# The first head pair's rows from three queues, and routing and shared rows over two groups

## The reference

```
q, k, v = heads(xn @ Wq.T), heads(xn @ Wk.T), heads(xn @ Wv.T)      # 16 heads of 16
scores  = q k^T / 4
gauss   = exp(-0.5 |x - position|^2 / scale^2)     # 8 splats per head, of q and of k
dir     = tanh((x - position) . direction)
splat   = (amp qg) kg^T + strength (amp qg qd) (kg kd)^T
std     = softmax(causal(scores)) v Wo
gsa     = softmax(causal(scores + sensitivity splat)) v Wo
attention = (1 - blend) std + blend gsa

s = sqrt(softplus(xn @ gate_w.T));  two experts of 16 by top-k(s + gate_b);  weights s / sum
each expert takes its first 128 tokens: silu(x W1) * (x W3) @ W2      # inner width 176
plus a shared expert of the same form over all tokens
```

## Time and profile before

| | |
|---|---|
| median of 3 runs | 376.65 us (376.22 to 376.99) |
| the profiled execution | 378.75 us, span 376.9 us |
| PE busy | 334.7 us, 89% |
| PE weight loads busy | 174.8 us, 46% |
| DVE busy | 230.7 us, 61% |
| ACT busy | 194.1 us, 51% |
| POOL busy | 65.7 us, 17% |
| mean granted clock of TensorE | 0.947 |

### The profile page before, as it was taken

One profiled execution on the slowest core, in us unless ns is written; L12 is line 12 of the kernel. 1 busy time (PEld: TensorE's weight loads), 2 busy tenths in 40 slices (PEclk: granted clock), 3 DMA queues, 4 the chain that ended last, 5 costly groups with the idle time before them and its releaser, 6 DMA issues.

```text
span 376.9 us, 6181 instructions
## 1 busy us (share of the span) xinstructions
PE 334.7 (89%) x2172; PEld 174.8 (46%) x2172; DVE 230.7 (61%) x614; ACT 194.1 (51%) x278; POOL 65.7 (17%) x82
## 2 busy tenths in 40 slices
PE   0999996788979999999999999999999999989965
PEld 0643663343345544554455445544554454335433
DVE  4555857587674665567556655766577558776222
ACT  1699824525414365436543654366346547767530
POOL 7200140400047530110111011102010007710000
PEclk9999768598979999999999999999999999999995
DMA  6408623304341354245655565547555525510011
GB/s 220 131 0 103 107 38 41 60 13 60 47 135 15 41 75 73 71 89 102 142 153 105 113 139 153 107 93 154 129 125 111 79 53 127 143 42 2 0 57 56
DMA packets 27330, 33.01 MB, mean 88 GB/s; under 512 B 6593, under 2 KB 20097, under 8 KB 27297
## 3 DMA queue, kind: packets, MB, share of 16 engines
q1 hardware_dynamic: 23745, 28.32, 37.4%
q0 software_dynamic: 2128, 4.22, 3.9%
q10 hardware_dynamic: 1424, 0.04, 0.2%
HBM read 15.60 MB, written 4.28 MB: 53 GB/s over the span
## 4 chain that ended last, share of the span: by engine, by line
PE 72%; DVE 14%; ACT 9%; issue 3%; DMA 1%; SPq 0%; DVEq 0%; ACTq 0%
PE ps L817 16%; PE ps L745 9%; PE ps L800 8%; PE ps L788 7%; PE ps L754 7%; PE ps L718 6%; ACT arena_p L636 6%; DVE mx L1093 5%; PE ps L676 4%; PE ps L773 2%; PE ps L695 2%; PE ps L758 2%; PE ps L791 2%; DMA acc<-in_x_dram 1%; ACT small L641 1%
## 5 line engine op out<-in xcount | busy, mean ns | idle before, releaser
L636 ACT ACTIVATE arena_p<-ps 128x1024 f32<-128x1024 f32 (+1 forms) x192 | 147.2, 811 | 79.4 <-PE ps L800 53.7
L1093 DVE TENSOR_REDUCE mx<-ps 128x1 f32<-128x512 f32 (+3 forms) x160 | 89.3, 590 | 33.2 <-PE ps L718 22.7
L817 PE MATMUL ps<-arena_p,v_full 128*32 128x512 f32 (+3 forms) x768 | 72.6, 496 | 0.6 <-ACT arena_p L636 0.6
L718 PE MATMUL ps<-stage 96*128 96x512 bf16 (+3 forms) x160 | 51.5, 362 | 7.1 <-DVE mx L1093 4.7
L788 PE MATMUL ps<-stage 98*128 98x512 bf16 (+1 forms) x192 | 51.9, 337 | 4.7 <-ACT arena_p L636 4.2
L800 PE MATMUL ps<-stage 98*128 98x512 bf16 (+1 forms) x192 | 47.4, 332 | 3.0 <-ACT arena_p L636 2.4
L641 ACT ACTIVATE small<-ps 128x176 f32<-128x176 f32 x24 | 7.6, 318 | 64.1 <-PE ps L745 64.1
L387 POOL DMA_INDIRECT wt<-xn_scratch,ids_sb x16 | 15.2, 951 | 133.2 <-PE ps L735 127.6
L817 PEld LDWEIGHTS ps<-arena_p,v_full 128*32 128x32 f32 x768 | 20.2, 110 | 35.4 <-issue 30.3
L754 PE MATMUL ps<-arena_o,small 88*128 88x256 f32 x96 | 27.4, 409 | 8.3 <-DVE small L1116 6.3
L788 PEld LDWEIGHTS ps<-stage 98*128 98x128 bf16 x192 | 18.8, 100 | 23.5 <-ACT arena_p L636 9.8
(11 more groups left out here) (193 smaller groups left out, 418.5 us busy)
## 6 DMA issues: line engine op xcount, KB each, us to landing
w_sb<-in_w_dram SPq DMA_DIRECT2D x16, 352.0 KB
stage<-split SPq DMA_DIRECT2D x48, 96.0 KB, 2.9
stage<-split SPq DMA_DIRECT2D x48, 64.0 KB, 2.7
arena_o<-in_w_dram SPq DMA_DIRECT2D x16, 176.0 KB
stage<-split SPq DMA_DIRECT2D x80, 32.0 KB, 2.5
ye_scratch<-wt SPq DMA_DIRECT2D x16, 128.0 KB, 1.8
stage<-split SPq DMA_DIRECT2D x32, 48.0 KB
acc<-in_x_dram SPq DMA_DIRECT2D x2, 512.0 KB, 4.6
```

Of the source, the lines that this page charges most:

```text
L636: A(to, ps[:, 1 + 2 * s:3 + 2 * s, off:CH], ACT.Exp, scale=SCALE).then_inc(done, 1)
L718: ins = M(b[:, 0:n1 - n0], lhs, ks[0:KR, pr, h, n0:n1], start=True, stop=not diag)
L817: ins = M(ps[c:c + 2 * HD, 0, off:CH], v_full[:, jb + s, g * GH + h, :], of, start=jb + s == 0, stop=end)
L1093: V.reduce_max(mx[:, it // TC, h, it % TC, pc:pc + 1], b[:, 0:n1 - n0], AX.X).then_inc(aux_free, 1)
```

## The change

- In PRO the gate's logits move from behind the features to the middle of the projections: four proj tiles, gate, four proj tiles, par, features, v.
- ACT's Exp of the gate moves into the features, behind `part1(2)`. On DVE `gate()` stands ahead of the parameters' copy, `plus_one()` between `rest_of(2)` and `rest_of(3)`, and `softplus()` behind the first `shift`.
- ACT issues the six rows of key features of group 0, the ones with the first parts first, between its v tiles. SP issues the twelve of the queries part by part.
- The branch's body moves from SP to POOL, behind POOL's thirds of halves 6 and 7; SP waits for `gaps_ready`, which POOL sends behind it, before any feature row of group 0.
- PE turns the first shift after one v tile instead of two. PRE1 has 4 maxima instead of 8; the other 12 are in slots 0 to 2 of group 0, four in each.
- Main loop: routing goes over slots 8 to 31 counted from the loop's start instead of 1 to 22; the shared tiles over slots 12 to 48 instead of groups 0 and 1, four each; the experts over slots 52 to 124 instead of groups 2 to 5, four each; the adds over slots 136 to 180. One step of four tiles' chains stands in every fourth slot: in the same slot `y` of tile n, `hT` of n + 1, `gu` of n + 2 and `xT` of n + 3. Before, one tile's steps followed each other by one to three slots.

```diff
         PRO = [("xnT", (k, tq)) for tq in range(NC) for k in range(KD)]
-        PRO += [("proj", (s, m, tc)) for m in range(KD) for s in range(2) for tc in range(NC)] + [("par", 0)]
+        PRO += [("proj", (s, 0, tc)) for s in range(2) for tc in range(NC)] + [("gate", 0)]
+        PRO += [("proj", (s, 1, tc)) for s in range(2) for tc in range(NC)] + [("par", 0)]
         PRO += [("feat", (s, tc, w)) for s in range(2) for tc in range(NC) for w in range(2)]
-        PRO += [("gate", 0)] + [("v", n) for n in range(NT // 2)]
+        PRO += [("v", n) for n in range(NT // 2)]
...
-        SG = 4
-        G0, G1 = 2, 6
-        EG = E // (G1 - G0)
...
-        LATER = 8
-        first_rest = [(n // 2, ("pre", t)) for n, t in enumerate(max1[LATER:])] + [(4, ("pre", ("shift", 1)))]
+        LATER = 4
+        first_rest = [(n // 4, ("pre", t)) for n, t in enumerate(max1[LATER:])] + [(4, ("pre", ("shift", 1)))]
         first_maxima = spread_late(max0, 5, 9) + [(12, ("shift", 0))] + spread_late(max1, 10, 20) + [(22, ("shift", 1))]
 
-        def chain(tasks, at):
-            return [(n + 12 * (f // 2), (k, at + f)) for f in range(4) for k, n in tasks[f % 2]]
-        SHARED = ((("sgu", 2), ("shT", 5), ("sy", 6)), (("sgu", 7), ("shT", 9), ("sy", 10)))
-        EXPERT = ((("xT", 0), ("gu", 2), ("hT", 5), ("y", 6)), (("xT", 5), ("gu", 7), ("hT", 9), ("y", 10)))
+        def chain(kinds, count, at):
+
+            return [(at + 4 * (n + step), (kind, n)) for step in range(3, -1, -1) for n in range(count) for kind in kinds[step:step + 1]]
+
+
+        S_ROUTE, S_SHARED, S_EXPERT, S_ADD = (8, 32), 8, 52, (136, 180)
+        long = [(at, t) for at, t in chain(("-", "sgu", "shT", "sy"), NT, S_SHARED) if t[0] != "-"]
+        long += chain(("xT", "gu", "hT", "y"), E, S_EXPERT)
+        long += spread([("route", k) for k in range(ROUTE)], *S_ROUTE)
+        long += spread([("add", (k, n)) for n in range(NT) for k in range(2)], *S_ADD)
+        AT = {t: at for at, t in long}
         PLAN = []
         for g in range(NG):
-            lists = [[(11, ("oT", 0))]]
+            lists = [[(11, ("oT", 0))], [(at - g * NSLOT, t) for at, t in long if at // NSLOT == g]]
             if g:
                 lists.append([(3, ("oT", 1))])
             else:
                 lists.append(first_rest)
             if g < NG - 1:
                 lists.append(maxima if g else first_maxima)
-            if g == 0:
-                lists.append(spread([("route", k) for k in range(ROUTE)], 1, 22))
-            if g < G0:
-                lists.append(chain(SHARED, g * SG))
-            elif g < G1:
-                lists.append(chain(EXPERT, (g - G0) * EG))
             if g == NG // 2:
...
-            if g == NG - 2:
-                lists.append(spread([("add", (k, n)) for n in range(TC) for k in range(2)], 12, 22))
             if g == NG - 1:
-                lists.append(spread([("add", (k, n)) for n in range(TC, NT) for k in range(2)], 1, 12))
...
+        def wait_parts(eng, at, part):
+
+            if part == 2:
+                eng.wait_ge(part_done[at], 1)
+            else:
+                eng.wait_ge((first_part, second_part)[part], at + 1)
...
-            for at in POOL_THIRDS:
-                if at == POOL_THIRDS[2]:
-                    pool.wait_ge(late_thirds, 1)
+            pool.wait_ge(wide_ready, 1)
+            needed = pool.value_load(wide[0:1, 0:1], min_val=0, max_val=1)
+            for at in POOL_THIRDS[0:2]:
                 third_of(at)
+            with pool.If(needed > 0):
+                for at in POOL_THIRDS[2:]:
+                    third_of(at)
+                for at in range(8):
...
+            pool.nop(nofuse=True).then_inc(gaps_ready, 1)
+
+            with pool.If(needed < 1):
+                pool.wait_ge(late_thirds, 1)
+                for at in POOL_THIRDS[2:]:
+                    third_of(at)
...
-            sp.wait_ge(wide_ready, 1)
             sp.wait_ge(zeros_out, 16)
-            sp.wait_ge(ones_in, 32)
-            needed = sp.value_load(wide[0:1, 0:1], min_val=0, max_val=1)
-            with sp.If(needed > 0):
-                for at in range(8):
...
+            sp.wait_ge(gaps_ready, 1)
             load_feature_row(sp, 0, 0, N_F - 1, f_in[0])
-            for at in range(4, 6):
-                sp.wait_ge(part_done[at], 1)
-            for j in range(12):
-                load_feature_row(sp, 0, 0, j, f_in[0])
+            for run in range(3):
+                for at in (4, 5):
+                    wait_parts(sp, at, run)
+                for h in range(GH):
+                    for w in range(2):
+                        load_feature_row(sp, 0, 0, 6 * h + 2 * run + w, f_in[0])
             shift_rows(-1, 0, 0)
-            for at in range(6, 8):
-                sp.wait_ge(part_done[at], 1)
-            for j in range(12, N_F - 1):
...
+                if tc == 0:
+                    act.wait_ge(gate_dve, 1)
+                    A(g_[2][:, :, :], g_[1][:, :, :], ACT.Exp, scale=-1.0).then_inc(gate_act, 1)
...
-            for n in range(NT // 2):
-                evacuate(("v", n))
+
+            def key_feature_rows(run):
+                for at in (6, 7):
+                    wait_parts(act, at, 2 - run)
+                for h in range(GH):
+                    load_feature_row(act, 0, 0, 12 + 3 * h + run, f_in[0])
+
+            key_feature_rows(2)
+            key_feature_rows(1)
+            evacuate(("v", 0))
+            key_feature_rows(0)
+            evacuate(("v", 1))
             act.wait_ge(gate_dve, 2)
             A(g_[4][:, :, :], g_[3][:, :, :], ACT.Ln).then_inc(gate_act, 1)
+            evacuate(("v", 2))
+            evacuate(("v", 3))
...
-            prologue(n_v + 1)
             aux(-1, ("shift", 0), 0)
-            prologue(n_v + 2)
-            prologue(n_v + 3)
+            for n in range(1, NT // 2):
...
+            gate()
+            n = PRO.index(("par", 0))
+            dve.wait_ge(pro_full, n + 1)
+            V.reduce_sum(bound[:, 0:H], ps[0:1, n % PB, 3 * P:4 * P].rearrange("p (h n) -> p h n", n=NS), AX.X)
+            V.tensor_copy(gT, ps[:, n % PB, 0:3 * P].rearrange("p (w c) -> p w c", w=3)).then_inc(pro_dve, 1)
+            dve.wait_ge(pro_dve, 2)
+            link(V.reduce_max(bound[:, H:H + 1], bound[:, 0:H], AX.X))
+            V.tensor_scalar(wide[:, :], bound[:, H:H + 1], SAFE / SCALE, None, ALU.is_gt).then_inc(wide_ready, 1)
+
             rest_of(2)
+            plus_one()
             rest_of(3)
             product(0)
...
             for t in max0:
                 aux(-1, t)
-            gate()
             aux(-1, ("shift", 0))
-            for t in PRE1[0:4]:
+            softplus()
+            for t in PRE1:
                 aux(-1, t)
-            plus_one()
-            for t in PRE1[4:]:
-                aux(-1, t)
-            softplus()
 
             V.memset(bound[:, 0:1], 0.0).then_inc(late_thirds, 1)
```

More of the change, by code:

```diff
@@ L289, in place @@
             return 5 + n % AB, n + 1
-        def group_of(kind, e):
-            return e // SG if kind in ("sgu", "shT", "sy") else G0 + e // EG
         def count_of(kind, e):
-            return place(group_of(kind, e), (kind, e))[1]
+            return place(AT[kind, e] // NSLOT, (kind, e))[1]
         def shape_of(ic, jb):
@@ L858, in _ @@
             prologue(n_v)
-            prologue(n_v + 1)
             aux(-1, ("shift", 0), 0)
-            prologue(n_v + 2)
-            prologue(n_v + 3)
+            for n in range(1, NT // 2):
+                prologue(n_v + n)
             for t in PRE1:
@@ L989, in row @@
                 return r.unsqueeze(2).to_broadcast((P, NT, E))
[L991 to L997 removed]
             def gate():
[L1000 removed]
+                n = PRO.index(("gate", 0))
+                dve.wait_ge(pro_full, n + 1)
+                V.tensor_copy(G[0], ps[:, n % PB, 0:NT * E].rearrange("p (n e) -> p n e", e=E)).then_inc(pro_dve, 1)
+                dve.wait_ge(pro_dve, 1)
                 V.scalar_tensor_tensor(out=G[1], in0=G[0], scalar=-1.0, in1=G[0], op0=ALU.mult, op1=ALU.max).then_inc(gate_dve, 1)
@@ L1163, in _ @@
             rest_of(7)
-            n = PRO.index(("gate", 0))
-            dve.wait_ge(pro_full, n + 1)
-            V.tensor_copy(G[0], ps[:, n % PB, 0:NT * E].rearrange("p (n e) -> p n e", e=E)).then_inc(pro_dve, 1)
             dve.wait_ge(wide_ready, 1)
@@ L1170, in _ @@
             with dve.If(needed > 0):
-                V.memset(bound[:, 0:1], 0.0).then_inc(late_thirds, 1)
                 V.memset(own_mx[:, :, :, :], 0.0).then_inc(own_read, 1)
```

47 lines of the change are left out of this document (19 added, 28 removed).

## The result

The changed kernel takes 387.0 us (384.4 to 393.4) where the kernel before takes 376.8 (376.2 to 377.8): ratio 1.0245, 95% interval 1.0181 to 1.0310. The forecast was 374.6 us with a range of 370.0 to 381.0, so it had the wrong sign, and the time lies outside the range. One of the four runs, 393.4 us, counts as slow and is left out of the ratio; the median of the other three is 386.1 us.

The account below looks back on a forecast made before the run. Bound by the prologue chain, then group 0, then PE-bound groups. Start +2.7, group 0 -5.6, one slot in four +1.2, adds -0.3 sum to -2.0 us: 374.6 us, 80% range 370.0 to 381.0.

Parts of the forecast that it names:

- The gate moved forward: Prologue: the gate amid the projections delays their second half, par and the features by 3.7 us.
- this rival: Projections: the gate halves the clock, making them up to 5.1 us late, 379.7 us in all; chance 0.18.
- plus_one: Prologue, DVE: waiting for the gate's Exp delays rest_of(3) and so ACT by 2.4 us more; last split over at 54.2.
- The branch on POOL: Prologue: the jump takes 2.8 us behind the last split at 54.2, so gaps_ready comes at 57.0 and SP's rows wait.
- it waits for the thirds: Upper bound for the branch on POOL: the jump starts only after POOL's thirds, with gaps_ready at 60.0.
- The rows and the shift: Prologue, SP: twelve query rows in 9.3 us, then the shift; first std 70.0, first pv 78.8, +2.7 us.
- the earlier transpose gains nothing: Prologue: turning the first shift earlier on PE gains nothing, because SP is busy for longer.
- Group 0: Main loop: half of 11.2 us excess recovered, -5.6 us, DVE 85% busy; ends 0 and -9.5.
- One slot in four: Main loop: chain steps in slot 0 of every pair make Tanh wait ahead of Exps, +1.2 us; upper bound +8.
- with the adds: Main loop: adds spread over two groups gain 0.3 us.
- just keeps up: New groups: SP has about 7.3 us between y steps for 3 expert DMAs and 4 to 8 rows, just enough.
- my four signs of being wrong: SP's rows before 52; clock 0.50 between 25 and 36; six-expert group over 45 us; PE awaiting a DMA before gu.

Follow-up runs that it names:

- e5: The changed kernel unchanged, run again for comparison: 387.5 us, ratio 1.0233 to the kernel before.
- e15: e14 with the gate logits mid-projections and plus_one ahead of the third rest, as in the change: 373.7 us, ratio 0.9893.
- e9: The changed kernel with the wide branch and its body back on SP: 418.7 us, ratio 1.0169, in a sitting with standstills.
- e10: e3, e7 and e8 together (gate back, shift early, experts and adds in old slots): 370.8 us, ratio 0.9819.
- e14: e10 with the wide branch and its body back on SP, as in e9: 371.2 us, ratio 0.9840.
- e6: The changed kernel with SP's twelve query rows in the order of the kernel before: 386.3 us, ratio 1.0221.
- e3: The changed kernel with the gate's logits, Exp, plus_one and softplus where they stood before, or nearly: 416.9 us, ratio 1.0108, in a sitting with standstills.
- e7: The changed kernel with the first shift issued behind SP's first four query rows: 422.8 us, ratio 1.0291, in a sitting with standstills.
- e12: The changed kernel with the experts' chain two slots later, in slot 2 of each pair: 423.5 us, ratio 1.0299, in a sitting with standstills.
- e8: The changed kernel with experts and adds back in their old slots, shared tiles and routing as in the change: 382.5 us, ratio 1.0145.
- e13: e10 with the change's own lists for experts and adds, and an expert's first weights loaded one pair earlier: 373.4 us, ratio 0.9880.
- e4: The changed kernel with plus_one behind rest_of(7) instead of ahead of rest_of(3): 422.6 us, ratio 1.0254, in a sitting with standstills.
- e2: The kernel before with only the new lists of the main loop: 417.9 us, ratio 1.0138, in a sitting with standstills.

## Why the prediction was wrong, by its own steps

**The gate moved forward: its cost right, the clock behind it wrongly left out of the sum.** I had 3.7 us for the gate, and it takes 3.5 where the clock stays up (e5). But the clock falls to 0.50 within the gate or up to 1 us behind it in all eleven profiles that have it in the middle of the projections, for 6.8 us in two (the change, e15) and for 3.4 in nine, and in none of the six others. That costs 3.4 or 1.7 us; the sum had nothing for it. I had argued against this rival with the dense matmuls on both sides of the gate; they did not keep the clock up. The projections ended 5.0 us later than before, and the last split 1.5 later than forecast. The Trainium skill's rule that I set beside it (TensorE: Matmul & The Clock Gate, Part 1), by which the low clock is the default and activity lifts it, agrees with the fall at 22.6 us. The gate also left a hole where it had been: PE stands for 5.9 us ahead of the first row maximum (51.30), behind ACT's last feature tile, which ends at 49.73. Where the gate stood before, its 32 matmuls filled time in which PE had nothing else to do.

**plus_one: right.** 2.4 us forecast, 2.41 measured.

**The branch on POOL: its price right.** I had `gaps_ready` 2.8 us behind the last split, with POOL's sequencer ahead of its thirds. It came at 58.50, 2.8 us behind the split at 55.65; the 57.0 of the forecast was too early only by the split. The upper case, "it waits for the thirds", is not what happens: the signal comes before their end. The rule of the Trainium skill that I cited (Runtime: NRT & Kernel Launch, Instruction fetch mechanics), by which a taken branch out of the fetched pages stops the sequencer, agrees with the 2.5 to 2.8 us on POOL and the 2.5 to 3.0 on SP; that it is the fetch that takes them, no run shows. I had SP's rows wait for this signal too; what I did not ask is what the branch's old place on SP would be worth beside late splits. On SP it stands ahead of work that needs only the query halves, and these are ready early; on POOL it stands behind the thirds of the keys' halves 6 and 7. All of SP's rows are thereby tied to the last split. e9 shows what that is worth with the splits late: 8 to 9 us of first pv. With the splits early (e10, e14) it is worth nothing that can be seen in the time.

**The rows and the shift: this step failed.** 9.3 us forecast for the twelve rows, 12.3 measured, with single issues of up to 2.6 us. ACT's rows are issued in the same microseconds; I called these hidden because ACT had time for them, and didn't ask what they might do to SP. That they are the cause is not shown (e6), so it stays open. The shift behind the rows I had right; that `mT` had been ready for 10.6 us stood in my text only as "the earlier transpose gains nothing". First std 73.8 instead of 70.0: 1.6 from the late gap row, 3.0 from the rows, less 0.8 since the shift landed sooner than I had it. First splat 77.4 instead of 72.0, first pv 82.0 instead of 78.8. From splat to pv it took 4.6 us, less than the 6.8 that I had.

Late split, branch, rows and shift are one series: undo the gate (e3), the branch (e9) or the shift's place (e7) alone, and the first pv comes at 73.6, 74.0 or 76.3 instead of 82 to 83. The three don't add up: all of them together give 73.6 (e14), and the gate and the shift without the branch 71.2 (e10). These are single profiles whose projections alone end at 26.96 to 28.74 us with the gate in its old place, so a difference of 2 us between two of them says little.

**Group 0: right in kind, too large in size.** Forecast 41.0 us, or -7.7; 44.2 in the profile, with 3.4 us at the low clock, and 42.5 in e5 and e10. The two waits of 1.75 and 2.17 us went, and where the clock stays at 1.00 6.2 us are gained. DVE is 71 to 72% busy there, not 85%.

**One slot in four: this step failed, and it is the largest miss.** I priced it at +1.2 us, with the adds +0.9, and looked for the cost in ACT's Tanh behind the Exp of std 0, whose place e12 changes without gain. The cost is 5.9 to 7.1 us (the first profile and e5 against e8). 2.9 to 4.1 are the shorter lead from `y(a)` to `gu(a + 3)` (e13); I had counted SP's issues, 7.3 us for the pair, and found that it "just keeps up", but not asked how long a load lies between the store that frees its buffer and the matmul that needs it. About 3 us stay open.

Three of my four signs of being wrong came: the clock at 0.50 between 25 and 36 us, a group of six experts over 45 us (45.5), and PE waiting for a DMA before `gu` (1.6 us, in e5 2.8).

Also open: what the standstills are, what slows SP's issues, and why e7's time doesn't show its earlier pv.

## What to carry to other kernels

Price a wait that is moved by what is queued behind it and by what it is now tied to, not by the instruction: the same branch moves the first pv by 8 us or costs nothing in the time, depending on how late the work ahead of it is. Two things that end together are told apart only by a run in which they don't, or by the order of their ends over many runs. When a chain of steps is respaced, compute for each buffer the slots from its release to its next use and set them against the load in the trace. If several edits sit in one series, undo each alone and all together before keeping any: here the change hid a version 1.8% faster than the kernel before.

## What the runs showed of the hardware

- The granted clock fell in the middle of PE's densest stretch, during or up to 1 us behind 3.6 to 4.1 us of 16-column matmuls with no idle time, in eleven of eleven profiles, for 3.4 or 6.8 us.
- While SP and ACT issue rows in the same microseconds, single issues of SP take 1.2 to 3.0 us instead of 0.7; the cause is not shown. In e10 ACT issues a row at 51.11 and one at 51.83, and SP's from 51.51 takes 2.96.
- The jump over the body of some 250 DMAs holds the sequencer for 2.5 to 3.0 us on SP and for 2.5 to 2.8 on POOL, while a POOL operation issued before it runs on. A signal that POOL's sequencer sends next comes before that operation is over (58.50 against 58.62 in the change, 58.11 against 58.41 in e7).
- A 0.23 us operation of DVE took 2.0 to 2.2 us beside POOL's (e4).
- The standstills: windows view of e2, in group 1, with no PE instruction while POOL issues its scatters at 0.96 us each as in other runs.

```profile
127.30:142.60 15.30, 0.00 (x0) 0.00 (x0) 1.03 (x3) 0.91 (x2) 9.45 (x10) 0.61 0.09 9
```
